# Maxima over the partitions: from a GpSimd instruction to a transposition, a row maximum and a product with ones

## The chip, the cores and the metric

One NeuronCore of a Trainium2 chip runs the whole program. Its engines are TensorE (PE in the profile), VectorE (DVE), ScalarE (ACT), GpSimd (POOL) and SyncE (SP), which only issues DMAs. They run side by side and meet at semaphores and at the barriers between blocks of code. The metric is the device time of one execution in microseconds.

## The reference

64 images of 224x224 are cut into 16x16 patches and projected to 196 tokens of 192 numbers. With a class token each image has 197 rows; 12,608 rows in all. Then come one attention layer with 12 heads, whose tensors are all rounded to 8-bit steps, and a layer of 8 experts (2 chosen per row):

```python
def fake_quant(x, n_bits=8):
    qmax = 2 ** (n_bits - 1) - 1
    scale = jnp.maximum(jnp.max(jnp.abs(x)) / qmax, 1e-08)
    q = jnp.clip(jnp.round(x / scale), -qmax - 1, qmax) * scale
    return x + jax.lax.stop_gradient(q - x)
...
qkv = jnp.einsum('bnc,oc->bno', fake_quant(x), fake_quant(w_qkv)) + b_qkv
attn = jnp.einsum('bhnd,bhmd->bhnm', fake_quant(q), fake_quant(k)) * scale
attn = jax.nn.softmax(attn, axis=-1)
out = jnp.einsum('bhnm,bhmd->bhnd', fake_quant(attn), fake_quant(v))
out = jnp.einsum('bnc,oc->bno', fake_quant(out), fake_quant(w_proj)) + b_proj
```

Each `fake_quant` needs one number: the largest absolute value of a whole tensor. On the chip a tensor lies over 128 partitions, so its maximum is first one number per partition, and then has to become one number that every partition knows. This last step is what the change is about. It is done four times, for eight numbers: three at once (input rows, two weight matrices), three at once (q, k, v), one (the smallest sum of exponentials, which sets the largest softmax value), one (the attention output).

## The kernel before

The program is a row of blocks with a barrier between each and the next:

- `embed`: patches to rows. GpSimd orders patches, TensorE transposes and multiplies.
- `normalise`: layer norm statistics, the first three maxima, rounding of weights (lines 560 to 637), then the rows are turned and q, k, v are computed once only for their maxima (`channels` on TensorE, `maxima` on VectorE), then the second three maxima.
- `attend_maxima`, called the score stage here: for 32 pairs of images ("couples") it makes q, k, v again, rounds q and k to integers on GpSimd (line 763), stores them, and computes all scores once, for the maximum and the sum of exponentials of every row. The second buffer lets couple n+1 be prepared during couple n.
- the first block of `attend`, called the shift block here: logarithms of the sums become a shift per row (line 1098), split in three bf16 parts (lines 1109 to 1116), turned by TensorE and written into q's rows in DRAM by many small DMAs.
- the second block of `attend`, called the attention stage: scores again, exponentials on ScalarE (line 1351, four buffers), rounding to 1/127 steps in turn by VectorE and GpSimd (line 1173; GpSimd takes units 1, 3, 5, 7 and 8 of the ten of a couple), products with v on TensorE. The last unit of a couple that uses `k_ends` waits for GpSimd's line 1234. SyncE issues in this order: loads of couples 0 and 1, the placing of the shifts of couples 4 to 31 (lines 1205 to 1207), q and k of couple 2, and v of couple 2 after couple 0 is through (line 1191), 24 more placings (lines 1209 to 1212), couple 3, and so on.
- `last_stages`, called the last block: projection, residual and norm, the gate and lists of rows per expert, the experts on lists, the weighted sum and the last norm. Every engine has its own long sequence in this one block. GpSimd starts with `plan_start` (lines 1855 to 1858) and the constants of lines 1549 to 1560; TensorE starts with waits for the constants (`init`), for VectorE's rounded bias (`bch`, line 1770) and for the first integers (`oq`).

In each of the four places the maximum over the partitions is `partition_all_reduce` on GpSimd. It stands at lines 464, 466, 1062 and 1250; VectorE waits for it in lines 594, 676, 1121 and 1402. The order of instructions in every engine is the order of the source; nothing rearranges it. Where GpSimd's stream goes from ordinary instructions to this one or back, the built program holds a configuration instruction, `MODIFY_POOL_CONFIG`, in the profile under the line of the instruction that follows it.

## Time and profile before

| | us |
|---|---|
| median of three executions | 2142.77 |
| lowest, highest | 2141.11, 2146.48 |
| the profiled execution, its own time | 2143.66 |
| its span in the trace | 2141.9 |
| PE busy in the span | 1530.5 |
| DVE busy | 1482.1 |
| ACT busy | 1361.9 |
| POOL busy | 1175.8 |

The span is the time from the first to the last instruction that the profiler recorded; 1.76 us of the execution's own time lie around it. In the rows below a line ends, in square brackets, with how long the engine was idle before the instruction and what released it. "issue" there means that the engine waited for nothing that the profile shows. The letters q in POOLq or SPq mark the sequencer of an engine, that is, instructions that are not counted as busy. Blocks begin at about these times: `normalise` 345, score stage 496, shift block 1030, attention stage 1049.6, last block 1330.

### The profile page before, as it was taken

To read this page: it belongs to the slowest core of one execution; us is meant where nothing else is said; L and a number is where in the kernel's file an instruction comes from. 1 tells how busy PE (TensorE), PEld (TensorE's weight loads), DVE (VectorE), ACT (ScalarE), POOL (GpSimd) and SP (SyncE) were. 2 spreads that over 40 slices of the span, in tenths; PEclk is the share of its full clock that TensorE was granted. 3 is DMA by queue.
4 is the path that set the end of the run, shared out by engine and by line. 5 is a ranking of instruction groups with operands and counts; after the bars stand their busy time and mean duration, and the time that the engine had idled before them with its cause. 6 is when DMAs were issued, how large, how long until landed. Compare 5 with 4: busy or idle time off the path is not lost. (4 is left out here: it accounts for less than half of the span.)

```text
span 2141.9 us, 51815 instructions
## 1 busy us (share of the span) xinstructions
PE 1530.5 (71%) x12460; PEld 1033.5 (48%) x12461; DVE 1482.1 (69%) x3737; ACT 1361.9 (64%) x3884; POOL 1175.8 (55%) x1921
## 2 busy tenths in 40 slices
PE   1999993884555555555378986788873999993663
PEld 1999992441111111111134443445542998883553
DVE  0455556896777777777456665688876777775996
ACT  0222221543999999999589996677772776663553
POOL 2333330004666666666155554377775888875886
PEclk9999996896555555555555555555556999997776
DMA  5334421001222222222344453544433555553774
GB/s 172 155 160 183 159 92 35 1 0 38 80 72 82 79 72 84 77 73 91 67 125 143 143 150 113 150 154 154 156 122 117 143 140 144 143 165 119 233 223 136
DMA packets 183979, 254.09 MB, mean 119 GB/s; under 512 B 28154, under 2 KB 147243, under 8 KB 180208
## 3 DMA queue, kind: packets, MB, share of 16 engines
q1 hardware_dynamic: 136256, 192.53, 29.2%
q0 software_dynamic: 19840, 39.17, 5.1%
q10 hardware_dynamic: 27808, 21.50, 3.1%
q8 instruction: 34, 0.56, 0.1%
q14 instruction: 41, 0.34, 0.1%
HBM read 140.66 MB, written 107.86 MB: 116 GB/s over the span
## 5 line engine op out<-in xcount | busy, mean ns | idle before, releaser
L957 ACT ACTIVATE exps_summed<-s,neg_shift 128x197 f32<-128x197 f32 x1184 | 482.7, 478 | 41.3 <-POOL neg_shift L824 39.7
L994 DVE TENSOR_REDUCE score_max<-s 128x788 f32 (+2 forms) x320 | 284.7, 894 | 108.9 <-PE s L898 96.7
L957 ACT ACTIVATION_READ_ACCUMULATOR exps_summed<-s,neg_shift (+1 forms) x1184 | 304.3, 260 | 0.0
L1351 ACT ACTIVATE exps<-st,scalars 128x788 f32<-128x788 f32 (+1 forms) x320 | 246.8, 889 | 21.1 <-PE st L1264 17.2
L2029 POOL DMA_INDIRECT expert_sums<-y_tile,row_places x216 | 215.6, 998 | 58.8 <-issue 28.2
L361 PE MATMUL mm<-w_tok,x_transposed 128*112 128x192 f32 x1344 | 239.6, 329 | 0.0
L306 ACT COPY x_transposed<-tp 128x672 f32<-128x672 f32 x112 | 80.4, 718 | 241.2 <-PE tp L352 241.2
L338 POOL TENSOR_SCALAR x_patches<-x_tile 112x768 f32<-112x768 f32 x112 | 93.1, 832 | 223.5 <-PE tp L352 184.8
L361 PEld LDWEIGHTS mm<-w_tok,x_transposed 128*112 128x112 f32 x1344 | 215.5, 179 | 0.2
L898 PE MATMUL s<-k_int,qk_int 16*128 16x197 bf16 x768 | 98.7, 354 | 139.9 <-ACT exps_summed L957 127.0
L1173 POOL TENSOR_SCALAR probs<-exps 128x788 bf16<-128x788 f32 (+1 forms) x160 | 130.3, 821 | 99.3 <-ACT exps L1351 99.2
L1173 DVE TENSOR_SCALAR probs<-exps 128x788 bf16<-128x788 f32 (+1 forms) x160 | 94.3, 590 | 112.0 <-ACT exps L1351 79.0
L392 DVE TENSOR_TENSOR h_rows_all<-mm,posb 112x192 f32<-112x192 f32 (+1 forms) x112 | 40.0, 357 | 178.7 <-PE mm L361 128.9
L824 POOL TENSOR_TENSOR neg_shift<-score_max,neg_alpha 128x4 f32<-128x4 f32 (+1 forms) x320 | 63.9, 200 | 136.0 <-DVE score_max L994 118.6
L1573 POOL DMA_INDIRECT listed_rows<-z_rows_a,row_index x99 | 103.3, 1043 | 60.9 <-DVE row_index L1755 31.9
L898 PEld LDWEIGHTS s<-k_int,qk_int 16*128 16x128 bf16 x768 | 26.0, 106 | 225.9 <-ACT exps_summed L957 215.7
L2122 ACT ACTIVATE g<-dn,down_bias 128x256 f32<-128x256 f32 x216 | 90.6, 470 | 68.4 <-PE dn L2071 67.3
L979 DVE TENSOR_SCALAR qkv_y<-pqk,scalars 128x394 f32<-128x394 f32 (+1 forms) x192 | 116.7, 608 | 24.5 <-POOL qk_int L763 21.3
L763 POOL TENSOR_SCALAR qk_int<-qkv_y,scalars 128x394 bf16<-128x394 f32 x96 | 122.4, 1275 | 17.9 <-issue 6.8
L2267 PE MATMUL weighted<-sum_a,weight_diagonals 128*128 128x192 f32 (+1 forms) x198 | 70.4, 449 | 83.6 <-DVE weight_diagonals L2321 60.2
L1573 POOL DMA_INDIRECT listed_rows<-z_rows_b,row_index x99 | 101.1, 1021 | 30.2 <-issue 27.8
L352 PE MATMUL tp<-ident_f,x_patches 112*128 112x112 f32 x672 | 85.1, 264 | 44.6 <-POOL x_patches L338 44.6
(403 smaller groups left out, 4561.9 us busy)
## 6 DMA issues: line engine op xcount, KB each, us to landing
x_tile<-in_x SPq DMA_DIRECT2D x24, 1568.0 KB
z_tile<-listed_rows SPq DMA_DIRECT2D x108, 196.0 KB
v_ints<-v_slots SPq DMA_DIRECT2D x32, 480.0 KB, 2.5
v_slots_in<-v_ints SPq DMA_DIRECT2D x32, 480.0 KB, 3.6
q_ints<-qk_int SPq DMA_DIRECT2D x32, 295.5 KB, 2.6
k_ints<-k_int SPq DMA_DIRECT2D x32, 295.5 KB, 2.5
q_shifted<-q_ints SPq DMA_DIRECT2D x32, 295.5 KB, 3.8
k_ones<-k_ints SPq DMA_DIRECT2D x32, 295.5 KB, 4.6
```

The costliest lines, as they stand in the source:

```text
L338: pool.tensor_scalar(xs[:, w % 2, :].rearrange("p (f w) -> p f w", w=PATCH), src, 1.0, 0.0, ALU.mult, ALU.add).then_inc(xs_ready, 1)
L361: last = nc.tensor.matmul(mm[w % 2][0:ROWS, 0:D], xt[:, w % 2, k * ROWS:(k + 1) * ROWS], w_tok[:, k, :], start=(k == 0), stop=(k == KCH - 1))
L763: pool.tensor_scalar(qk[:, s, g], y[:, g % 2], p.col(C_MQ), None, ALU.subtract).then_inc(used, 1)
L898: ins = nc.tensor.matmul(o[:, 2 * b + m, 0:SEQ], qk[lo:lo + HD, s, g, m * SEQ:m * SEQ + 128], kk[lo:lo + HD, s, g, m * SEQ:(m + 1) * SEQ], ...
L957: act.activation(gone[:, v % 2, k], ps[v % 3][:, k, 0:SEQ], ACT.Exp, scale=alpha, bias=nb[:, s, to:to + 1], accum_out=p.lsum[:, bass.ds(n ...
L979: dve.tensor_scalar(y[:, f % 2, 0:w], pqk[:, f % 2, 0:w], p.col(C_CQK if f < GRP else C_CV), p.col(C_MQ), ALU.mult, ALU.add).then_inc(y_re ...
L994: dve.tensor_reduce(columns(m, u), src, op=ALU.max, axis=AXL.X).then_inc(max_done, 1)
L1173: eng.tensor_scalar(pr[:, s, at(u):at(u) + size(u), 0:SEQ], ex[:, v % 4, 0:size(u)], 1.0, 128.0, ALU.mult, ALU.add).then_inc(sem, 1)
L1351: act.activation(ex[:, v % 4, 0:size(u)], src, ACT.Exp, scale=alpha, bias=p.col(C_LNSA)).then_inc(e_ready, 1)
L1573: pool.indirect_dma_start(p.zs[:, :], bass.IndirectOffsetOnAxis(ap=idx[0:rows, s, 4 * a + t:4 * a + t + 1], axis=0), z[0:rows, s, t, :], N ...
L2029: pool.indirect_dma_start(p.yD[:, :], bass.IndirectOffsetOnAxis(ap=to[:, k, t:t + 1].bitcast(U32), axis=0), y[:, k, t, :], None, bounds_ch ...
L2122: act.activation(g[:, k % 2, m], pd[k % 2][:, m], ACT.Gelu, scale=1.0 / WSCALE, bias=p.db[:, bass.ds(e * 2 + m, 1)]).then_inc(gs, 1)
```

## The change

Three helpers replace `partition_all_reduce`. `turn_maxima` has TensorE transpose the column of per-partition maxima (128 partitions by n) into n rows of 128 in PSUM. `reduce_maxima` has VectorE take the maximum of each row, and multiply an n by n identity with it, which gives a diagonal. `spread_maxima` has TensorE multiply a 3 by 128 tile of ones with that diagonal, so that all 128 partitions of PSUM hold the n maxima; the instruction on VectorE that used the result now reads it from PSUM. All four places are changed in this way, a PSUM bank is added in `normalise` and in the shift block, and GpSimd has no block of its own left in these two.

```diff
+def turn_maxima(nc, p, bank, values, n, sem):
+    nc.tensor.transpose(bank[0:n, 0:128], values, p.idf[:]).then_inc(sem, 1)
+
+def spread_maxima(nc, p, bank, n, sem):
+    nc.tensor.matmul(bank[:, 128:128 + n], p.ones3[0:n, :], p.diag[0:n, 0:n], start=True, stop=True).then_inc(sem, 1)
+
+def reduce_maxima(dve, p, bank, n, link, row):
+    link(dve.tensor_reduce(p.col(row, 0, n), bank[0:n, 0:128], op=ALU.max, axis=AXL.X))
+    link(dve.tensor_scalar(p.diag[0:n, 0:n], p.idf[0:n, 0:n], p.col(row, 0, n), None, ALU.mult))
...
+        self.ones3 = sb("ones_f32", [3, 128], f)
+        self.diag = sb("maxima_diagonal", [3, 3], f)
...
                 pool.tensor_copy(p.idb[:], p.idf[:]).then_inc(id_s, 1)
+                pool.memset(p.ones3[:], 1.0).then_inc(id_s, 1)
...
+        bank = p.ps("maxima", [128, 512], F32, c)
...
-            @block.gpsimd
-            def _(pool):
-                pool.wait_ge(max_ok, 1)
-                pool.partition_all_reduce(p.sc[:, C_ZMAX:C_ZMAX + 3], pm[:], 128, RMAX).then_inc(red, 1)
-                pool.wait_ge(max_ok, 2)
-                pool.partition_all_reduce(p.sc[:, C_QM:C_QM + 3], pm[:], 128, RMAX).then_inc(red2, 1)
...
             def _(pe):
+                pe.wait_ge(max_ok, 1)
+                turn_maxima(nc, p, bank, pm[:], 3, red)
+                pe.wait_ge(max_ok, 2)
+                spread_maxima(nc, p, bank, 3, red)
                 pe.wait_ge(w_ok, 1)
...
                     channels(NG - 1, d)
+                pe.wait_ge(max_ok, 3)
+                turn_maxima(nc, p, bank, pm[:], 3, red2)
+                pe.wait_ge(max_ok, 4)
+                spread_maxima(nc, p, bank, 3, red2)
...
                 dve.wait_ge(red, 1)
-                link(dve.tensor_scalar(p.sc[:, C_SX:C_SX + 3], p.sc[:, C_ZMAX:C_ZMAX + 3], 1.0 / QMAX, FLOOR, ALU.mult, ALU.max))
+                reduce_maxima(dve, p, bank, 3, link, C_TOP)
+                dve.sem_inc(max_ok, 1)
+                dve.wait_ge(red, 2)
+                link(dve.tensor_scalar(p.sc[:, C_SX:C_SX + 3], bank[:, 128:131], 1.0 / QMAX, FLOOR, ALU.mult, ALU.max))
...
+            bank = p.ps("smallest", [128, 512], F32, c)
...
-                @block.gpsimd
-                def _(pool):
-                    pool.wait_ge(low, 1)
-                    pool.partition_all_reduce(p.col(C_LMIN), p.col(C_TMP), 128, RMAX).then_inc(red, 1)
...
                 def _(pe):
+                    pe.wait_ge(low, 1)
+                    turn_maxima(nc, p, bank, p.col(C_TMP), 1, red)
+                    pe.wait_ge(low, 2)
+                    spread_maxima(nc, p, bank, 1, red)
                     for j, (lo, hi) in enumerate(spans):
...
                     link(dve.reciprocal(p.col(C_IALPHA), p.col(C_NALPHA)))
+                    dve.wait_ge(red, 1)
+                    reduce_maxima(dve, p, bank, 1, link, C_TOP)
+                    dve.sem_inc(low, 1)
                     for j, (lo, hi) in enumerate(spans):
...
-                            dve.wait_ge(red, 1)
+                            dve.wait_ge(red, 2)
-                            link(dve.tensor_scalar(p.col(C_TMP), p.col(C_LMIN), -1.0, None, ALU.mult))
+                            link(dve.tensor_scalar(p.col(C_TMP), bank[:, 128:129], -1.0, None, ALU.mult))
...
                     for sem in over:
                         pool.sem_clear(sem)
-                    pool.wait_ge(chain, 2)
-                    pool.partition_all_reduce(p.col(C_OM), p.col(C_TMP), 128, RMAX).then_inc(red, 1)
...
                     products_high(COUPLES - 1, 1)
+                    pe.wait_ge(chain, 2)
+                    turn_maxima(nc, p, pb, p.col(C_TMP), 1, red)
+                    pe.wait_ge(chain, 4)
+                    spread_maxima(nc, p, pb, 1, red)
...
                     dve.wait_ge(red, 1)
-                    quantise_inverse(dve, link, p.col(C_SO), p.col(C_IO), p.col(C_OM))
+                    reduce_maxima(dve, p, pb, 1, link, C_TOP)
+                    dve.wait_ge(red, 2)
+                    quantise_inverse(dve, link, p.col(C_SO), p.col(C_IO), pb[:, 128:129])
```

In the shift block ScalarE's `act.wait_ge(low, 2)` becomes `low, 3`, and VectorE's transposed-row maximum stands ahead of line 1098.

The first place is GpSimd's stream at the start of the score stage. Before:

```order
87 L771 COPY x_ends<-xq_t 128x2x60
88 L770 COPY x_ends<-xq_t 67x128
89 L771 COPY x_ends<-xq_t 67x2x60
90 L763 ISA
91 L763 TENSOR_SCALAR qk_int<-qkv_y,scalars 128x394 x3
92 L778 TENSOR_TENSOR q_ends<-qk_int,q_rows 128x3x4x5 x2
```

After:

```order
83 L798 COPY x_ends<-xq_t 128x2x60
84 L797 COPY x_ends<-xq_t 67x128
85 L798 COPY x_ends<-xq_t 67x2x60
86 L790 TENSOR_SCALAR qk_int<-qkv_y,scalars 128x394 x3
87 L805 TENSOR_TENSOR q_ends<-qk_int,q_rows 128x3x4x5 x2
```

L763 is now L790. The `ISA` row ahead of the rounding to integers, the configuration instruction, is gone; the other rows are the same.

The second place is GpSimd's stream from the end of the attention stage to the start of the last block. The 56 rows in one are the clearing of semaphores. Before:

```order
344 L1248 ISA x56
345 L1250 ISA
346 L1250 ISA scalars<-scalars 128x1
347 L1176 UNCONDITIONAL_BRANCH
348 L2438 UNCONDITIONAL_BRANCH
349 L1855 ISA
350 L1855 IOTA tile_number 1x108
351 L1856 MEMSET pad_rows 128x392
```

After:

```order
333 L1203 TENSOR_SCALAR probs<-exps 128x4x197
334 L1278 ISA x56
335 L1206 UNCONDITIONAL_BRANCH
336 L2472 UNCONDITIONAL_BRANCH
337 L1889 IOTA tile_number 1x108
338 L1890 MEMSET pad_rows 128x392
339 L1892 MEMSET pad_rows 128x2
```

Three `ISA` rows are gone: the configuration, the reduction itself, and the configuration ahead of `tile_number`. At the start of the attention stage the row ahead of `k_ends<-k_ones,k_rows` (L1234, now L1264) is gone in the same way, and in the shift block nothing of GpSimd is left.

The third place is VectorE at the end of the attention stage, where the maximum of the output is made. Before:

```order
1075 L1380 TENSOR_REDUCE out_max<-channels_t 128x1
1076 L1400 TENSOR_REDUCE scalars<-out_max 128x1
1077 L1401 TENSOR_SCALAR scalars<-scalars 128x1
1078 L182 TENSOR_SCALAR scalars<-scalars 128x1
1079 L183 RECIPROCAL scalars<-scalars 128x1
1080 L1404 TENSOR_TENSOR scalars<-scalars 128x1
```

After:

```order
1082 L1432 TENSOR_REDUCE scalars<-out_max 128x1
1083 L1433 TENSOR_SCALAR scalars<-scalars 128x1
1084 L198 TENSOR_REDUCE scalars<-po_rest 1x1
1085 L199 TENSOR_SCALAR maxima_diagonal<-ident_f,scalars 1x1
1086 L182 TENSOR_SCALAR scalars<-po_rest 128x1
1087 L183 RECIPROCAL scalars<-scalars 128x1
```

Two instructions stand between the last one before the reduction (L1401, now L1433) and its first user (L182): the row maximum, which waits for TensorE's transposition, and the diagonal, for which TensorE's product waits. `po_rest` is the PSUM tile that this place shares. The other three places have the same two rows.

## Rows read from the trace of the kernel before

Times are microseconds from the start of the span; L763 is line 763 of the kernel before.

**Rows 1.** The page: the chain of waits that ended last, by engine.
```profile
PE 17%; DVE 7%; issue 5%; POOL 4%; DMA 3%; ACT 1%; DVEq 0%; SPq 0%; POOLq 0%; ACTq 0%
```

**Rows 2.** The chain in order of time: start, duration (us), what; its longest piece.
```profile
1330.27 7.85 issue
```

**Rows 3.** By line: GpSimd's configuration instructions (ns, then first to last start, us).
```profile
L763 POOLq MODIFY_POOL_CONFIG  x2: 8/8/8, 503.9 to 503.9; - x2
L1855 POOLq MODIFY_POOL_CONFIG  x2: 11/11/11, 1330.2 to 1330.3; - x2
```

**Rows 4.** Timeline: start, duration (us), instruction, [idle before and releaser].
```profile
363.97 0.17 DVE L595 TENSOR_SCALAR scalars<-scalars 128x3 f32<-128x3 f32 x1 [0.61 <-POOL scalars L464]
...
493.23 0.23 DVE L678 TENSOR_SCALAR scalars<-scalars 128x3 f32<-128x3 f32 x1 [0.56 <-POOL scalars L466]
```

**Rows 5.** Timeline at the start of the score stage.
```profile
510.64 3.81 POOL L763 TENSOR_SCALAR qk_int<-qkv_y,scalars 128x394 bf16<-128x394 f32 x3 [6.76 <-issue]
```

**Rows 6.** Timeline at the start of the shift block.
```profile
1031.81 0.15 DVE L1093 TENSOR_SCALAR scalars<-scalars 128x1 f32<-128x1 f32 x1
1032.61 0.37 DVE L1098 SCALAR_TENSOR_TENSOR shift<-shift,scalars,score_max 128x148 f32<-128x148 f32 x1 [0.35 <-DVE scalars L1095]
1035.05 0.16 DVE L1111 CAST last_parts<-shift_rest 128x4 bf16<-128x4 f32 x1
1035.32 0.09 PEld L1085 LDWEIGHTS last_t<-ident_bf,last_parts 128*12 128x12 bf16 x1 [9.12 <-DVEq L1116]
1036.81 0.15 DVE L1123 TENSOR_SCALAR scalars<-scalars 128x1 f32<-128x1 f32 x1
```

**Rows 7.** Timeline of the first image pairs of the attention stage.
```profile
1054.04 4.15 ACT L1351 ACTIVATE exps<-st,scalars 128x788 f32<-128x788 f32 x5 [2.62 <-PE st L1264]
1060.59 0.53 POOL L1234 TENSOR_TENSOR k_ends<-k_ones,k_rows 128x60 bf16<-128x60 bf16 x2 [10.04 <-issue]
...
1062.05 4.46 ACT L1351 ACTIVATE exps<-st,scalars 128x788 f32<-128x788 f32 x6 [3.87 <-POOL probs L1173]
```

**Rows 8.** Timeline, later: SyncE's DMA issues and TensorE.
```profile
1066.85 0.43 SPq L1189 DMA_DIRECT2D k_ones<-k_ints  x1
...
1072.33 0.33 SPq L1192 DMA_DIRECT2D v_slots_in<-v_ints  x1
1072.70 12.23 SPq L1031 DMA_DIRECT2D q_ints<-shift_last  x24
...
1089.09 0.85 PE L1264 MATMUL st<-q_shifted,k_ones 32*128 32x197 bf16 x12 [7.86 <-DMA k_ones<-k_ints]
```

**Rows 9.** Timeline at the end of attention.
```profile
1325.49 0.21 DVE L1401 TENSOR_SCALAR scalars<-scalars 128x1 f32<-128x1 f32 x1
1328.72 0.15 DVE L182 TENSOR_SCALAR scalars<-scalars 128x1 f32<-128x1 f32 x1 [3.01 <-POOL scalars L1250]
```

**Rows 10.** Timeline at the start of the last block.
```profile
1335.77 0.41 DVE L1770 SCALAR_TENSOR_TENSOR w_proj_q<-b_proj_parts,ident_f 3x192 bf16<-3x192 bf16 x1
1340.63 0.29 POOL L1560 TENSOR_SCALAR_AFFINE_SELECT lower_index<-lower_index 128x64 f32<-128x64 f32 x1
1341.18 0.32 PE L1630 MATMUL proj<-w_proj_q,o_int 128*128 128x192 bf16 x1 [18.25 <-POOL lower_index L1560]
```

**Rows 11.** Timeline: prices of a row maximum, a transposition, small products.
```profile
360.39 0.27 DVE L583 TENSOR_REDUCE class_stats<-row_tmp 112x1 f32<-112x112 f32 x1
...
1349.85 0.48 PE L1677 MATMUL z_tp<-ident_f,z_rows_a 128*128 128x128 f32 x1 [0.98 <-ACT z_rows_a L1603]
...
1358.12 1.77 PE L1645 MATMUL gate_l<-gate_w,gate_hidden 96*128 96x8 f32 x8
```

**Rows 12.** Stretches: busy us (instructions) of each engine, granted clock, DMA share.
```profile
369.70:391.00 21.30, 16.80 (x73) 10.60 (x74) 15.32 (x40) 10.26 (x22) 0.00 (x0) 0.51 0.01 1
391.00:493.00 102.00, 81.49 (x489) 45.45 (x487) 99.65 (x176) 42.48 (x87) 0.17 (x1) 1.00 0.00 1
493.00:1640.00 1147.00, 757.22 (x6680) 338.92 (x6680) 820.36 (x1967) 931.00 (x3022) 695.12 (x1371) 0.50 0.34 107
```

More of the change, by code:

```diff
@@ L239 @@
  C_IQ, C_IK, C_IV, C_CQ, C_CK, C_CV, C_ALPHA, C_NALPHA, C_LMIN, C_SA, C_LNSA, C_IALPHA, C_SAV, C_OM, C_SO,
- C_IO, C_CO, C_SOUT, C_TMP, C_MQ, C_CQK, C_MIN, C_EPS, C_ISOUT, C_ONES) = range(41)
+ C_IO, C_CO, C_SOUT, C_TMP, C_MQ, C_CQK, C_MIN, C_EPS, C_ISOUT, C_ONES, C_TOP) = range(42)
 def embed(p):
@@ L676, in _ @@
                 dve.wait_ge(red2, 1)
+                reduce_maxima(dve, p, bank, 3, link, C_TOP)
+                dve.sem_inc(max_ok, 1)
+                dve.wait_ge(red2, 2)
                 s3 = p.sc[:, C_SQ:C_SQ + 3]
-                link(dve.tensor_scalar(s3, p.sc[:, C_QM:C_QM + 3], p.col(C_SXW), 1.0 / QMAX, ALU.mult, ALU.mult))
+                link(dve.tensor_scalar(s3, bank[:, 128:131], p.col(C_SXW), 1.0 / QMAX, ALU.mult, ALU.mult))
                 link(dve.tensor_scalar(s3, s3, FLOOR, None, ALU.max))
@@ L1073, in _ @@
                             place_last(act, a, k, 1, 0, at_first[1])
-                    act.wait_ge(low, 2)
+                    act.wait_ge(low, 3)
                     act.activation(p.col(C_LNSA), p.col(C_SA), ACT.Ln).then_inc(lnd, 1)
```

## The prediction, made before the run

> **What bounds the kernel now.** I read the page first: no engine is busy all through, so what matters is what is waited for at each place. The chain of waits that ended last gives PE 17%, DVE 7% and "issue" 5% [rows 1], and of its pieces the longest is of the last kind: 7.85 us from 1330.27 [rows 2], right behind a configuration instruction of GpSimd at 1330.2 to 1330.3 [rows 3]. So I read GpSimd's configuration instructions by line, then the timeline around each, and last the other waits for the reduction. A configuration instruction shows 8 to 11 ns [rows 3], but behind it GpSimd stands still for some 7 to 10 us, and the profile names no releaser [rows 2, 5, 7]. The reader is to look for who is behind GpSimd in each place: that alone is time.
>
> **Part by part.** Everything is in the time of the profiled execution, 2143.66 us.
>
> (a) Start of the score stage. GpSimd has copied the row ends at 503.9, has its configuration instruction then [rows 3], and starts to round q and k at 510.64, 6.76 us later with "issue" as reason [rows 5]. All that follows (k's DMAs, the first scores, the first exponentials on ScalarE) hangs on these three roundings. "issue" says that its input was there; VectorE's first two results do not wait for GpSimd, so nothing else is late when the stall goes: -6.76. Bounds: -7.0 (the whole of it and the start of the next) and -5 (if the third input, which needs a buffer back from GpSimd, comes late once the roundings run close).
>
> (b) Start of the attention stage. `k_ends` is at 1060.59, after 10.04 us of "issue" behind the configuration instruction of line 1234 [rows 7]. Its input k has landed before 1054, since ScalarE's first exponential of scores made from it starts at 1054.04 [rows 7]. ScalarE does five exponentials and then has no free buffer, since GpSimd has not rounded its unit: it waits 3.87 us, until 1062.05 [rows 7]. Without the stall GpSimd's `k_ends` (0.53) is done near 1054, before its first rounding is due, so ScalarE's wait goes: -3.87. What is late next? TensorE waits 7.86 us for couple 3's k at 1089.09 [rows 8]. That looks like an end that would swallow the gain. But SyncE's v load at 1072.33 is issued when couple 0's last product is through, 24 placings then take 12.23 us, and only then couple 3 is loaded [rows 8]. That product comes 3.87 earlier, so this chain moves with it, unless SyncE becomes late by itself: its load of couple 2's k is over at 1066.85 + 0.43 = 1067.28, 5.05 us ahead of 1072.33, so 3.87 fits [rows 8]. I take -3.87; bounds 0 (all swallowed) and -5.0 (up to where SyncE itself sets the time).
>
> (c) Start of the last block. GpSimd's constants end at 1340.63 + 0.29 = 1340.92, and TensorE starts at 1341.18 for that reason [rows 10]. The stall ends at 1330.27 + 7.85 = 1338.12 [rows 2], so 2.8 us of work stand behind it. Without it they end near 1333.1. Then VectorE's bias chain is last: it ends at 1335.77 + 0.41 = 1336.18 [rows 10], and TensorE can start 0.1 later, at 1336.3. So -4.9, not -7.85. Everything behind it (projection, norm, gate, lists) is relative to this start.
>
> (d) The round trip that is added. No row shows it whole, so I add it from pieces at TensorE's lower clock of 1.2 GHz, which holds in three of the four places [rows 12]: VectorE's end to TensorE's start 0.11 (1035.21 to 1035.32, [rows 6]); a transposition with 128 columns of f32 0.48 [rows 11]; back 0.05; maximum of 128 elements 0.27 (112 elements, [rows 11]) and link 0.04; the diagonal 0.21, as for another one-column product with a scalar from memory [rows 9], and link 0.04; to TensorE 0.11; a product of few columns 0.25 (eight take 1.77, [rows 11]); back 0.05. The sum is 1.61. Bounds: 1.2 if the pieces overlap (clock at 2.4 GHz, weight load before the wait ends), 2.6 if every crossing costs 0.3 us more than its nearest row, as the 0.35 at line 1098 shows that waits can [rows 6]. This is set against what VectorE waits now:
> - first maxima: 0.61 now [rows 4], so +1.00. Here the configuration had been done while VectorE worked, nothing is gained there.
> - second maxima, at the higher clock: 1.61 - 0.21 for the transposition = 1.40 against 0.56 [rows 4]: +0.84.
> - end of attention: VectorE ends at 1325.70 and goes on at 1328.72, a wait of 3.01 that also holds the tail of a configuration [rows 9]. 3.02 - 1.61: -1.41.
> - shift block: now VectorE goes from line 1120 to 1123 (1036.81) without an idle [rows 6], the reduction costs nothing. After the change VectorE waits for the transposition before line 1098: from 1031.96, 0.11 + 0.48 + 0.05 + 0.31 + 0.25 gives 1033.16, and with the wait for the logarithm checked after it some 0.15 more, against 1032.61: +0.70. Behind this wait in VectorE's queue are all of the block's splits, and TensorE's turns and the DMAs wait for those, so it counts in full. The product with ones lies beside VectorE's splits, as does ScalarE's wait for `low`.
>
> (e) The memset of the ones (about 0.1) lies before GpSimd's first wait for the patches; the two PSUM banks cost no time.
>
> Sum: -6.76 - 3.87 - 4.9 + 1.00 + 0.84 - 1.41 + 0.70 = -14.4. From 2143.66 this gives 2129.3. The median shown is 0.9 lower than the profiled execution; from it I get 2128.4, and I say **2128.5**.
>
> Two rules of the Trainium skill speak to this. In this trace the gaps from the configuration to the next work are 6.7, 10.0 and 7.9 us for (a), (b) and (c) [rows 3, 5, 7, 10]. The page "GPSIMD Engine Reference", section "Instruction dispatch", puts the first call to a freshly loaded kernel at about 6 us (5.95). By that figure 0.8 us of (a)'s gap would be something else and might stay, and the sum would be -13.6; in (b) and (c) there would still be enough time, as another end is reached first. And the same page's "When to use GPSIMD" names GpSimd as the only option for a reduction across partitions, which speaks against the whole change; for the instruction alone the trace agrees (0.56 to 0.61 us of waiting against an estimate of 1.4 to 1.6), and the change would then be a loss of 0.8 to 1.0 at each place if the configuration cost nothing.
>
> **Rivals.**
> 1. The attention stage takes the gain of (b) back: SyncE's DMA issues or the landing of couple 2's and 3's k are the real end. For it: TensorE waits 7.86 us for k at 1089.09 [rows 8]. Against it: the issue before that wait is itself released by TensorE. (b) is then 0, or the round trips come near their upper bound (4 x 1.0): sum -10.5, and both together -6.5. Time 2132 to 2136.
> 2. The stalls move instead of going: GpSimd needs a configuration for another instruction in place of these (`iota`, the masks, the power in the last norm). Against it: the order after the change shows no such row, and `iota` stands there among ordinary instructions. If one stall of 7 us stayed: -7.5, time 2135.
> 3. More than forecast: SyncE issues its placings behind an earlier start and (b) reaches -5.0, the round trips cost 1.2 (-1.6), and stages after it are met earlier by DMAs: -17 or more, time 2126 and below.
> 4. Slower than before: the clock. TensorE runs `normalise` from 369.7 to 391 at half clock and from 391 to 493 at full [rows 12]. The two small products now come before its block work, and if the rise came late or not at all, TensorE would bound this stage: 81.5 us of its busy time in 102 would become 163, so up to +61, or 0.6 us lost for each us that the rise is late. From a rise 24 us later on this outweighs the 14.4, and with none the time is 2143.7 - 14.4 + 61 = 2190. Against it: the rise came after 21 us of dense work, the new products are two small ones ahead of it, and nothing of the dense work changes.
>
> **How the numbers follow.** The forecast has 0.66, rival 1 0.17, rival 2 0.04, rival 3 0.09, rival 4 0.02; 0.02 are left for a run-to-run difference that hides it. The three executions before lie 5.4 us apart, so the median itself is uncertain by some 2 us. A measurement of this kernel can tell about 0.3%, 6.4 us, from no change: faster means below 2136.3. Forecast, rival 1's larger part and rival 3 lie there, 0.92; within 0.3%: 0.05; slower 0.03. The forecast's own range, from the bounds of (d) (+1.6 to -1.6 for four places, and +4.0 at worst) and the executions' spread, is 2124 to 2133; to hold 8 in 10 I take in most of rival 1 and some of rival 3: 2122 to 2135.
>
> **What would show it.** In the profile after the change: no configuration instruction after the first few us; the rounding to integers starting within 0.3 us of the last copy of row ends; no wait of ScalarE for GpSimd near the sixth exponential of the attention stage, and couple 3's first score some 3.9 us nearer to the stage's start; TensorE's first projection released by VectorE's line 1770 (now 1804), about 6.0 us after the block's start (1330.3 before) instead of 10.9; VectorE's pause before its user of the maximum near 1.6 us in all where it was 0.61, 0.56 and 3.01, and the first line of the shift split 0.7 later. The forecast is wrong if couple 3 starts at the same distance from the stage's start, if a pause around a maximum is above 2.6 us, or if the granted clock rises elsewhere.

## The result, and the profile after

| | before | after |
|---|---|---|
| median (executions) | 2144.85 us (8) | 2127.80 us (8) |
| lowest, highest | 2140.43, 2148.04 | 2122.70, 2136.76 |
| profiled execution, its span | 2143.66, 2141.9 | 2127.63, 2125.9 |

The ratio is 0.9926, with a 95% interval of 0.9911 to 0.9942: faster by 0.74%, 16 us at 2144.85 (the two medians are 17.0 apart). The forecast was 2128.5, from a difference of 14.4.

The two timelines, cut at the same instructions; "again" is a second profile of the same changed kernel, from a later comparison (E5):

| stretch, us | before | after | again | forecast change |
|---|---|---|---|---|
| start to normalise's class statistics | 355.8 | 353.0 | 356.5 | 0 |
| to the first scale (holds the first maxima) | 8.2 | 9.4 | 9.3 | +1.00 |
| to the last row maximum of normalise | 127.4 | 126.4 | 128.5 | 0 |
| to the second scale (second maxima) | 1.8 | 2.7 | 3.1 | +0.84 |
| score stage: GpSimd's first memset to its first q integers | 14.15 | 8.05 | 8.05 | -6.76 |
| q integers to the shift block | 519.8 | 518.8 | 518.8 | 0 |
| shift block to its first shift line | 2.2 | 2.8 | 2.8 | +0.70 |
| attention stage: first memset to the output's maximum | 275.6 | 270.9 | 270.1 | -3.87 |
| output's maximum to its scale | 3.5 | 2.3 | 2.2 | -1.41 |
| to TensorE's first projection | 12.5 | 7.9 | 7.9 | -4.9 |
| projection to the end | 800.7 | 803.5 | 803.2 | 0 |

Two stretches between these rows are not shown, 3.3 us ahead of the score stage and 17 us behind the first shift line; they differ by 0.4 at most. The seven rows with a forecast add to -13.8 in the first profile and to -14.4 in the second. The rows without one differ by up to 3.5 us between two profiles of one kernel (353.0 and 356.5), so the -16.0 of the spans is -13.8 and scatter. Part of the scatter is TensorE's clock: in the second profile it was granted at half between 482 and 488 us, in the first at full there, and the stretch to the last row maximum is 128.5 us in place of 126.4.

By line, GpSimd's configuration instructions. One pair is left, at the program's start; those of [rows 3] at lines 763 and 1855 are gone, and so are the ones that the kernel before has at lines 464, 1062, 1234 and 1250:

```profile
L335 POOLq MODIFY_POOL_CONFIG  x2: 11/11/11, 1.1 to 1.2; - x2
```

Timeline (start, duration, instruction, [idle before and releaser]) at the start of the score stage, the place of [rows 5]:

```profile
495.21 5.83 DVE L997 CAST k_int<-scalars 128x1182 bf16<-128x1182 f32 x2
...
497.12 3.29 POOL L780 MEMSET v_slots<- 128x3840 bf16 x1
...
501.10 0.51 PE L889 MATMUL pqk<-xq_t,w_slots 128*128 128x394 bf16 x1 [9.60 <-DVE k_int L997]
...
502.85 3.80 POOL L790 TENSOR_SCALAR qk_int<-qkv_y,scalars 128x394 bf16<-128x394 f32 x3 [0.69 <-DVE qkv_y L1006]
```

The 6.76 us of "issue" are gone. What GpSimd waits for now is VectorE's first result, 0.69. That is late because TensorE waited for VectorE's two casts, which take 5.83 us here.

ScalarE, SyncE and TensorE in the first image pairs of the attention stage, answering to [rows 7, 8]. The first line is TensorE's wait for couple 2's k in the kernel before:

```profile
1073.26 1.02 PE L1264 MATMUL st<-q_shifted,k_ones 32*128 32x197 bf16 x12 [0.61 <-DMA k_ones<-k_ints]
```

The changed kernel:

```profile
1045.68 14.47 ACT L1383 ACTIVATE exps<-st,scalars 128x788 f32<-128x788 f32 x19 [2.56 <-PE st L1292]
...
1060.00 0.33 SPq L1222 DMA_DIRECT2D v_slots_in<-v_ints  x1
1060.37 11.82 SPq L1058 DMA_DIRECT2D q_ints<-shift_last  x24
...
1064.18 0.85 PE L1292 MATMUL st<-q_shifted,k_ones 32*128 32x197 bf16 x12 [3.86 <-DMA k_ones<-k_ints]
...
1076.09 0.84 PE L1292 MATMUL st<-q_shifted,k_ones 32*128 32x197 bf16 x12 [4.20 <-DMA k_ones<-k_ints]
```

ScalarE does 19 exponentials in a row; before, it did 5 and then waited 3.87 us for GpSimd. SyncE's v load comes 18.7 us after the stage's start at 1041.3, where it was 1072.33 - 1049.6 = 22.7. The 24 placings follow as before, and couple 3 starts 34.8 after the start, where it was 39.5. TensorE's waits for k are now 3.86 us for couple 2 and 4.20 for couple 3, where they were 0.61 and 7.86. So TensorE does wait longer for couple 2, but couple 3 sets the time, and it comes sooner.

The pauses around the maxima on VectorE, first and second place, answering to [rows 4]:

```profile
360.44 0.15 DVE L613 TENSOR_TENSOR partition_max<-partition_max,class_stats 64x1 f32<-64x1 f32 x1
...
362.37 0.16 DVE L619 TENSOR_SCALAR scalars<-maxima 128x3 f32<-128x3 f32 x1 [0.73 <-PE maxima L193]
...
489.90 0.16 DVE L698 TENSOR_TENSOR partition_max<-class_stats 128x1 f32<-128x1 f32 x1
...
491.54 0.22 DVE L705 TENSOR_SCALAR scalars<-maxima,scalars 128x3 f32<-128x3 f32 x1 [0.53 <-PE maxima L193]
```

From the end of the last line ahead of each pause to its user VectorE has 362.37 - 360.59 = 1.78 us and 491.54 - 490.06 = 1.48 us, where it waited 0.61 and 0.56.

The same at the end of attention, with TensorE, answering to [rows 9]:

```profile
1312.50 0.21 DVE L1433 TENSOR_SCALAR scalars<-scalars 128x1 f32<-128x1 f32 x1
1312.77 0.37 PE L188 MATMUL po_rest<-ident_f,scalars 128*1 128x128 f32 x1 [2.83 <-DVE scalars L1433]
1313.25 0.28 DVE L198 TENSOR_REDUCE scalars<-po_rest 1x1 f32<-1x128 f32 x1 [0.54 <-PE po_rest L188]
1313.56 0.20 DVE L199 TENSOR_SCALAR maxima_diagonal<-ident_f,scalars 1x1 f32<-1x1 f32 x1
1313.82 0.58 PE L193 MATMUL po_rest<-maxima_diagonal,ones_f 1*128 1x1 f32 x2 [0.68 <-DVE maxima_diagonal L199]
1314.51 0.16 DVE L182 TENSOR_SCALAR scalars<-po_rest 128x1 f32<-128x1 f32 x1 [0.75 <-PE po_rest L193]
```

From 1312.71 to 1314.51: 1.80 us, where it was 3.02. The product with ones is two passes (x2), 0.58 us.

VectorE in the shift block, answering to [rows 6]:

```profile
1023.03 0.15 DVE L1120 TENSOR_SCALAR scalars<-scalars 128x1 f32<-128x1 f32 x1
...
1024.45 0.37 DVE L1128 SCALAR_TENSOR_TENSOR shift<-shift,scalars,score_max 128x148 f32<-128x148 f32 x1 [0.16 <-DVE maxima_diagonal L199]
```

The first shift line comes 1.27 us after the line before the pause; in [rows 6] it was 0.65. The added 0.62 is what the row maximum and the diagonal hold VectorE.

The start of the last block, answering to [rows 10]:

```profile
1317.17 0.51 DVE L1723 TENSOR_SCALAR o_y<-channels_t,scalars 128x512 f32<-128x512 f32 x1
1317.60 0.47 DVE L1724 TENSOR_SCALAR o_y<-channels_t,scalars 64x512 f32<-64x512 f32 x1
...
1319.29 0.37 POOL L1594 TENSOR_SCALAR_AFFINE_SELECT lower_index<-lower_index 128x64 f32<-128x64 f32 x1
...
1321.92 0.41 DVE L1804 SCALAR_TENSOR_TENSOR w_proj_q<-b_proj_parts,ident_f 3x192 bf16<-3x192 bf16 x1
1322.43 0.32 PE L1664 MATMUL proj<-w_proj_q,o_int 128*128 128x192 bf16 x1 [8.03 <-DVE w_proj_q L1804]
```

GpSimd's constants end at 1319.66, 2.8 us before TensorE starts, and VectorE's bias chain releases TensorE now. From the output's scale to the end of that chain it is 7.8 us, where it was 7.5: the two roundings in it (lines 1727 and 1728) take 0.51 and 0.63 us in place of 0.43 and 0.41, with GpSimd writing its constants beside them. E4 has the same two times; E1 to E3, where the constants come later, have 0.43 and 0.41.

The first stretch of [rows 12] (busy us and instructions of PE, PEld, DVE, ACT, POOL; granted clock; DMA share; GB/s):

```profile
369.70:391.00 21.30, 16.07 (x78) 10.08 (x78) 16.07 (x41) 11.39 (x24) 0.00 (x0) 0.62 0.01 1
```

The clock rose somewhat sooner: 0.62 of full in this stretch against 0.51 makes some 5 us, of which 1.6 are the earlier first scale. Rival 4, a late rise, did not occur.

### The profile page after: what moved, and what is told of

It is laid out like the page before. It is cut to its first block and busy times, and to the rows that moved or that the text cites. A ratio compares the mean times of both kernels' runs of the same rounds, so it can differ in the third digit from the quotient of the medians.

```text
span 2125.9 us, 51836 instructions
## 1 busy us (share of the span) xinstructions
PE 1531.2 (72%) x12472; PEld 1032.7 (49%) x12473; DVE 1486.6 (70%) x3745; ACT 1361.7 (64%) x3884; POOL 1176.2 (55%) x1918
## 5 line engine op out<-in xcount | busy, mean ns | idle before, releaser
L790 POOL TENSOR_SCALAR qk_int<-qkv_y,scalars 128x394 bf16<-128x394 f32 x96 | 122.4, 1275 | 11.8 <-DVE qkv_y L1006 5.7
L1006 DVE TENSOR_SCALAR qkv_y<-pqk,scalars 128x394 f32<-128x394 f32 (+1 forms) x192 | 116.7, 608 | 14.8 <-POOL qk_int L790 11.5
```

Of the source, the lines that this page charges most:

```text
L790: pool.tensor_scalar(qk[:, s, g], y[:, g % 2], p.col(C_MQ), None, ALU.subtract).then_inc(used, 1)
L1006: dve.tensor_scalar(y[:, f % 2, 0:w], pqk[:, f % 2, 0:w], p.col(C_CQK if f < GRP else C_CV), p.col(C_MQ), ALU.mult, ALU.add).then_inc(y_re ...
```

## Experiments

Theory: the gain is GpSimd's standstill behind a configuration instruction, and it counts in each place by what is queued behind it; the round trips cost about 1 us each. Rivals: the gain comes from the removed instruction itself or from the clock; the parts act only together; SyncE's order takes it back.

E1 to E4 ran on one chip, against 31 executions of the kernel before with a median of 2306.06 us. On that chip every kernel is some 160 us longer, and in the four profiles taken there this lies behind TensorE's first projection: in E3's it is at 1336.0 us and the rest takes 966 us, against 801. The stretches ahead of it match the other profiles, with the exceptions told under E4, so I read these four by stretch, and their ratios within the chip.

**E1, the instruction back, its result unused.**

```diff
+                pool.wait_ge(max_ok, 1)
+                pool.partition_all_reduce(p.unused[:], p.idf[:, 0:3], 128, RMAX).then_inc(spare, 1)
...
```

> The changed kernel, but GpSimd also runs a partition_all_reduce of a constant at each of the four old places, and nobody uses or waits for its result; the maxima still go by TensorE and VectorE. Theory (the gain is the configuration instruction that GpSimd meets when it returns to ordinary work while someone is queued behind it): MODIFY_POOL_CONFIG comes back at the first q integers of the score stage, at the first k_ends of the attention stage and at the start of the last block, each with some 6 to 7 us of wait; the three markers grow by 6, 4.6 and 4.5 us, the round trips stay as in the changed kernel, so about +15 us over it: 2143, ratio to the kernel before 0.997 to 1.003. Rival (the gain is the removed instruction and its wait for the maxima, or the clock): the time stays near 2128, ratio 0.993.

Ratio 0.9995 (0.9982 to 1.0008). GpSimd's timeline:

```profile
512.99 3.81 POOL L799 TENSOR_SCALAR qk_int<-qkv_y,scalars 128x394 bf16<-128x394 f32 x3 [7.45 <-issue]
...
1063.87 0.53 POOL L1278 TENSOR_TENSOR k_ends<-k_ones,k_rows 128x60 bf16<-128x60 bf16 x2 [10.47 <-issue]
...
1339.38 0.22 POOL L1905 IOTA tile_number<- 1x108 f32 x1 [8.54 <-issue]
```

The three standstills are back (7.45, 10.47 and 8.54 us), with nobody waiting for a result. From stage start to q integers 14.8 us; attention stage 274.7; output scale to first projection 13.3. The whole gain is gone, though the new way is all there: neither the wait for the reduction's result nor the clock is the gain. This run brings back the reduction together with the configuration, so it doesn't part the two; E10 below does. In the second of the three standstills, not all is the configuration: `k_ends` also needs k, as it does in [rows 7]. TensorE's first scores in the kernel before, made from the same k, start 7.1 us ahead of the `k_ends` of 1060.59:

```profile
1053.48 0.84 PE L1264 MATMUL st<-q_shifted,k_ones 32*128 32x197 bf16 x12 [5.51 <-DMA k_ones<-k_ints]
```

**E2, E3, E4, one part at a time.** The new way stands in normalise's two places alone (E2), in the shift block alone (E3), or at the end of attention alone (E4, whose edit is shown); the others keep `partition_all_reduce`.

```diff
-                    pool.partition_all_reduce(p.col(C_OM), p.col(C_TMP), 128, RMAX).then_inc(red, 1)
+                    pe.wait_ge(chain, 2)
+                    turn_maxima(nc, p, pb, p.col(C_TMP), 1, red)
+                    pe.wait_ge(chain, 4)
+                    spread_maxima(nc, p, pb, 1, red)
```

> The kernel before with the new way only in the two places of normalise. Theory: the score stage starts 6.1 us sooner, the two maxima cost 1.2 and 0.9 us more, net -4.0 us: 2141, ratio 0.998; the configuration waits of the attention stage and of the last block are as before. Rival: the parts act together (GpSimd needs to be free of the old instruction altogether), nothing is gained here: 2145 or, with the dearer maxima, 2147.

Ratio 0.9977 (0.9961 to 0.9993). GpSimd's first q integers follow its copies without an idle, 7.3 us after the stage's start:

```profile
503.50 3.82 POOL L790 TENSOR_SCALAR qk_int<-qkv_y,scalars 128x394 bf16<-128x394 f32 x3
```

> The kernel before with the new way only in the shift block. Theory: the attention stage's first couples are 4.6 us shorter, the shift block 0.65 us longer, net -4.0 us: 2141, ratio 0.998. Rival (SyncE's order sets the first couples, and what ScalarE gains it waits again for couple 2's k): the attention stage is shorter by under 1 us, net 0: 2145, ratio 1.000.

Ratio 0.9974 (0.9958 to 0.9990). The attention stage takes 270.5 us; `k_ends` comes with its data. TensorE at couple 3:

```profile
1081.60 0.85 PE L1287 MATMUL st<-q_shifted,k_ones 32*128 32x197 bf16 x12 [4.57 <-DMA k_ones<-k_ints]
```

The wait was 7.86 in [rows 8]. SyncE's order did not swallow the gain, but it leaves 4.57. In this run GpSimd's standstill at the start of the last block, which the edit doesn't touch, is the longest:

```profile
1332.91 0.22 POOL L1878 IOTA tile_number<- 1x108 f32 x1 [11.99 <-issue]
```

Its configuration instruction is at 1322.53, 10.4 us before; in [rows 2, 3] it is 7.9 us. From output scale to projection E3 has 15.0 us, where the kernel before has 12.5. Why this one took longer was not found.

> The kernel before with the new way only at the end of the attention stage. Theory: the pause for the attention output's maximum is 1.8 us instead of 3.0, and the last block's first projection comes 4.5 us sooner, net -5.7 us: 2139, ratio 0.9973. Rival (TensorE's start in the last block waits for something else by then): only the 1.2 us of the pause, 2143.5, ratio 0.9995.

Ratio 0.9969 (0.9953 to 0.9986). VectorE's scale and TensorE's first projection:

```profile
1326.85 0.16 DVE L182 TENSOR_SCALAR scalars<-po_rest 128x1 f32<-128x1 f32 x1 [0.75 <-PE po_rest L193]
...
1334.77 0.32 PE L1655 MATMUL proj<-w_proj_q,o_int 128*128 128x192 bf16 x1 [8.03 <-DVE w_proj_q L1795]
```

From output scale to projection 7.9 us. The three ratios multiply to 0.9922; the whole change gave 0.9926 and, below, 0.9932. Each of the three has an interval of about 0.0016 to either side, so the parts add as far as these times can tell. Each stretch is shorter only where its own part is done. The others stay within 1 us, but for a standstill that can take longer by itself: the 15.0 us in E3.

E5 to E8 ran on a chip on which the kernel before has a median of 2145.86 us (11 executions).

**E5, the changed kernel again** (no edit).

> The changed kernel once more, as the yardstick for the three beside it. Theory: ratio to the kernel before 0.992 to 0.9935, if the four places act one by one (the product of the parts tried alone, with their round trips, is 0.992). Rival (the parts overlap): 0.990 or 0.995.

2132.09 us, ratio 0.9932 (0.9915 to 0.9948), inside what was expected. Its stretches are in the table above.

**E6, GpSimd's long memset later.**

```diff
-                pool.memset(vs[:], 0.0).then_inc(zero, 1)
...
                 stamps(0, 0)
+                pool.memset(vs[:], 0.0).then_inc(zero, 1)
+                pool.wait_ge(zero, 5)
```

> The changed kernel with GpSimd's memset of v_slots (3.29 us) moved behind the first three integer steps of the score stage. Theory (what is left of the start is VectorE's two casts, 5.83 us instead of 2.08 because they run beside GpSimd's memsets): the casts fall to 2 to 3 us, TensorE's first product comes at about 2.6 us after the stage's start instead of 6.3, and the first q integers about 3.6 us sooner, -3.5 us over the changed kernel, ratio to before 0.991. Rival (the casts are slow for another reason, as the read of one broadcast column): they stay at 5.8 us and nothing moves but GpSimd's own memset, 0 us.

2129.05 us, ratio 0.9926 (0.9913 to 0.9939). VectorE's casts and GpSimd's integers:

```profile
496.15 2.61 DVE L998 CAST k_int<-scalars 128x1182 bf16<-128x1182 f32 x2
...
500.56 3.81 POOL L789 TENSOR_SCALAR qk_int<-qkv_y,scalars 128x394 bf16<-128x394 f32 x3 [0.69 <-DVE qkv_y L1007]
```

The casts fall from 5.83 to 2.61 us and the q integers come 3.2 us sooner (4.8 after the start). But the first exponential of the stage comes only 1.9 sooner (16.2 after the start against 18.1), since GpSimd's v values and first shifts now stand behind the memset; the whole from stage start to shift block is 525.6 against 526.8. The mechanism is right, but nearly two thirds of its gain are given back, and the times of E5 and E6 can't be told apart.

**E7, couples 2 and 3 asked for earlier.**

```diff
+                    place_rows((0, 1))
+                    load_qk(1, 0)
+                    place_rows((2, 3))
+                    place_lasts((0,))
+                    load_v(1, 0)
+                    load_qk(1, 1)
+                    place_lasts((1, 2, 3))
+                    load_v(1, 1)
```

> The changed kernel with SyncE's order changed in the attention stage: q and k of couple 2 are asked for after half of the placings, q and k of couple 3 before 18 of the last 24. Theory (after the change SyncE's order is the next bound of these first couples): the waits of 3.86 and 4.20 us for k_ones before couples 2 and 3 go, -7 to -8 us over the changed kernel, ratio to before 0.989. Rival (the placings that now come later are waited for before couple 4, or the other engines can't follow): the two waits move to couple 4, gain under 2 us, 0.992.

2127.72 us, ratio 0.9920 (0.9907 to 0.9933). Between the two: the attention stage is 267.1, 3.0 to 3.8 shorter than in the two profiles of the changed kernel. Couple 2's wait is gone. SyncE and TensorE for couples 3 and 4:

```profile
1068.35 0.43 SPq L1223 DMA_DIRECT2D k_ones<-k_ints  x1
...
1075.55 0.84 PE L1309 MATMUL st<-q_shifted,k_ones 32*128 32x197 bf16 x12 [2.48 <-DMA k_ones<-k_ints]
...
1085.52 0.85 PE L1309 MATMUL st<-q_shifted,k_ones 32*128 32x197 bf16 x12 [2.27 <-DMA k_ones<-k_ints]
```

k of couple 3 is asked for at 1068.35 and is there at 1075.55: 7.2 us, where the changed kernel has 1072.65 to 1076.09, 3.4. The load stands among the placings' DMAs; that these make it land late is likely, but was not tried by itself. Couple 4, which needs all placings, has a wait that it did not have. SyncE's order was the next bound, but it can be moved only in part.

**E8, first maxima by GpSimd, a memset behind.**

```diff
+                pool.partition_all_reduce(p.sc[:, C_ZMAX:C_ZMAX + 3], pm[:], 128, RMAX).then_inc(red, 1)
+                pool.memset(p.unused[:], 0.0).then_inc(spare, 1)
```

> The changed kernel, but the first three maxima come from partition_all_reduce on GpSimd again, with a small memset right behind it, while GpSimd has 130 us of nothing ahead. Theory (the configuration costs only where ordinary work is queued behind it): MODIFY_POOL_CONFIG is back in normalise, but nobody waits; the pause of VectorE before the first scale is 0.6 us instead of 1.78; the score stage starts as in the changed kernel; -1.2 us, ratio 0.992. Rival (the configuration is paid once more at the next ordinary instruction after a barrier): the score stage is 6 us later again, ratio 0.995.

2132.45 us, ratio 0.9939 (0.9926 to 0.9952). What was expected of the memset was wrong:

```profile
361.96 0.39 POOL L485 PARTITION_ALL_REDUCE scalars<-partition_max  x1 [38.35 <-DVEq L617]
362.22 0.17 POOL L486 MEMSET unused_max<- 128x3 f32 x1
...
362.38 0.17 DVE L619 TENSOR_SCALAR scalars<-scalars 128x3 f32<-128x3 f32 x1 [0.62 <-POOL scalars L485]
...
509.90 3.81 POOL L790 TENSOR_SCALAR qk_int<-qkv_y,scalars 128x394 bf16<-128x394 f32 x3 [6.83 <-issue]
```

VectorE's pause is 0.62 as expected, but the memset ran at once, 0.26 us behind the start of the reduction, and the configuration is by line in front of the q integers again:

```profile
L790 POOLq MODIFY_POOL_CONFIG  x2: 10/10/10, 503.1 to 503.1; - x2
```

So a memset does not bring the configuration back, and the 6.83 us are paid as before.

**E10, the same with a small tensor_scalar behind** (with E9 on a chip where the kernel before has 2143.43 us).

```diff
-                pool.memset(p.unused[:], 0.0).then_inc(spare, 1)
+                pool.tensor_scalar(p.unused[:], p.idf[:, 0:3], 1.0, None, ALU.mult).then_inc(spare, 1)
```

> The first maxima by partition_all_reduce as in the hybrid before, but the small instruction behind it is a tensor_scalar of three columns instead of a memset. In that hybrid the memset ran at once and the configuration stayed in front of the first q integers. Theory (a memset and a copy run in either configuration, a tensor_scalar needs the one it was built for): the configuration now stands in front of the small tensor_scalar, some 6 us inside GpSimd's 130 us of nothing, the score stage starts 8.1 us after its barrier as in the changed kernel, VectorE's first pause stays 0.6 us; -1.2 us over the changed kernel, ratio to before 0.992. Rival (it is loaded again at the first long instruction of each block): the score stage starts 14 us after its barrier, ratio 0.9945.

2128.26 us, ratio 0.9921 (0.9908 to 0.9934). GpSimd's timeline:

```profile
361.44 0.39 POOL L485 PARTITION_ALL_REDUCE scalars<-partition_max  x1 [38.36 <-DVEq L617]
368.91 0.79 POOL L486 TENSOR_SCALAR unused_max<-ident_f 128x3 f32<-128x3 f32 x1 [7.08 <-issue]
...
503.47 3.80 POOL L790 TENSOR_SCALAR qk_int<-qkv_y,scalars 128x394 bf16<-128x394 f32 x3
```

Now the standstill of 7.08 us lies in GpSimd's idle time, and the integers start 7.4 us after the stage's start with no idle. With it the reduction is there and the gain is too: the price is not the reduction, but who is queued behind the configuration. The old instruction can stay in a place if the way back is made early. The pause of 0.61 against 1.78 us at the first maxima is seen in the timeline, not in the times, whose interval is wider than that.

**E9, a version made of what was found.** ScalarE writes the ones of `k_int` and the zeros of `v_slots`, the loads are ordered as in E7, the gate's weights come after the last couple, GpSimd writes the ones of `o_int`.

```diff
+                for s in range(2):
+                    act.activation(kk[:, s].rearrange("p g t -> p (g t)"),
+                                   p.col(C_ONES).broadcast_to([128, GRP * 2 * SEQ]), ACT.Copy).then_inc(filled, 1)
+                for s in range(2):
+                    act.activation(vs[:, s], p.col(C_ONES).broadcast_to([128, VW]), ACT.Copy, scale=0.0).then_inc(filled, 1)
...
-        link(dve.memset(oq1[D1:KB], 1.0))
```

> The changed kernel with four more edits: ScalarE, idle there, writes the ones of k_int and the zeros of v_slots at the start of the score stage (VectorE's casts and GpSimd's long memset go); SyncE asks for q and k of couples 2 and 3 earlier, as tried before, and for the gate's weights only after the last couple's loads instead of before the placings; GpSimd writes the ones of o_int in the last block. Theory (the next bounds are those the runs showed: GpSimd's and VectorE's fills, SyncE's order, VectorE's bias chain): first q integers 4.5 us sooner than in the changed kernel, attention stage 4 to 7 us shorter (the waits of 2.5 us before couple 3 and 2.3 us before couple 4 that the earlier order left shrink, since the placings start 3.5 us sooner), last block 0.9 us sooner; together -9 to -12 us, ratio to before 0.987 to 0.9885. Rival (only moved: ScalarE's fills reach into its first exponentials, the loads stay behind the placings in the DMA queue): -4 us, 0.9905.

2117.14 us, ratio 0.9877 (0.9859 to 0.9895). It beats the kernel before by 1.2% and the changed kernel too, whose intervals (0.9911 to 0.9942 and 0.9915 to 0.9948) lie above. Rows of ScalarE and GpSimd at the start of the score stage, and of VectorE at the start of the last block:

```profile
499.79 2.27 ACT L974 ACTIVATE k_int<-scalars 128x1182 bf16<-128x1182 f32 x2 [25.98 <-PEq L467]
...
502.14 3.80 POOL L789 TENSOR_SCALAR qk_int<-qkv_y,scalars 128x394 bf16<-128x394 f32 x3
...
1312.17 0.84 DVE L1743 TENSOR_SCALAR o_y<-channels_t,scalars 128x512 f32<-128x512 f32 x1 [0.54 <-PEq L1207]
1312.93 1.06 DVE L1744 TENSOR_SCALAR o_y<-channels_t,scalars 64x512 f32<-64x512 f32 x1
```

The q integers start 2.9 us after the stage's start (8.1 in the changed kernel), and 4.7 of the 5.2 us are left at the shift block (522.1 against 526.8). The attention stage is 267.3, 2.8 to 3.6 shorter than in the changed kernel, less than the 4 to 7 expected; asking for the gate's weights later only changed where the waits are (2.84 before couple 3, 1.44 before couple 4). The last block gained nothing: VectorE's memset of 0.91 is gone, but its next two instructions take 0.84 and 1.06 us in place of 0.51 and 0.47, 0.92 more in all, beside GpSimd's memsets. These stretches hold 7 to 8 us; the median lies 10.5 to 12 below the changed kernel's, and where the rest is was not found.

## Why the prediction was right

The mechanism and the sum were right: -14.4 forecast, -13.8 and -14.4 in two profiles. E1 to E4 and E10 show that it was for the reasons given. That the time itself came within 0.7 us of 2128.5 is in part luck: the median before that it was counted from, 2142.77 of three executions, is 2144.85 with eight, and some steps came out larger and some smaller than forecast. By its steps:

- **(a) score stage**, -6.76 forecast, -6.1 measured at the q integers in both profiles. The standstill went whole (E2: 14.15 to 7.30, 6.85). The forecast said that nothing else would be late, and that the rounding would start within 0.3 us of the last copy; it was 0.69, for VectorE's first result. The neighbour that was overlooked is the cast of `k_int`, 2.08 us before and 5.83 after. What it costs doesn't last: from the stage's start to the shift block it is 533.9 us before and 526.8 in both profiles, -7.1, and 526.7 in E2, where the q integers are 0.75 sooner.
- **(b) attention stage**, -3.87 forecast, -4.7 and -5.5 measured, the second beyond the bound of -5.0 (E3 has -5.1). The chain was as told: ScalarE's wait goes, couple 0's product and with it SyncE's v load come 4.0 sooner, 24 placings, couple 3. The rest of the first profile's 4.7: the placings take 11.82 in place of 12.23, and couple 3's k is there 3.4 us after it is asked for, 0.3 less. Rival 1 did not occur: TensorE's wait for couple 2's k grew by 3.3 us and couple 2 comes only 0.8 sooner after the stage's start, but couple 3, behind which no such wait follows, comes 4.7 sooner. E7 shows its resource as the next bound.
- **(c) last block**, -4.9 forecast, -4.5 measured, released by the bias chain as forecast. The chain is 0.36 longer beside GpSimd's constants, which the step had left out.
- **(d) round trip**, 1.61 forecast, 1.78, 1.48 and 1.80 measured in the first profile, 1.78, 1.79 and 1.71 in the second. The second place was reckoned at the full clock, 1.40; in the second profile the clock had fallen back to half by the time of the product with ones (0.58 us there, 0.38 in the first), so this place is dearer than forecast, +0.91 and +1.23 for +0.84. The pieces differ more than the sum: transposition 0.37 (0.48 forecast), product with ones 0.58 (0.25 forecast, as one pass; the rows show two). The shift block has +0.62, +0.70 forecast. That GpSimd's instruction is the quicker one by itself is right too: 0.62 in E8, 0.61 in E10.
- **The old pause at the end of attention.** The way to the reduction needs a configuration too. It is at 1322.59 in the kernel before, and the reduction starts 5.6 us later, 2.5 after its input:

```profile
1328.23 0.38 POOL L1250 PARTITION_ALL_REDUCE scalars<-scalars  x1 [9.04 <-issue]
```

  This tail, which the step named, is why VectorE's pause was 3.01 there and 0.6 in normalise, and why the round trip by itself is a gain in this place alone.
- **The clock.** One sign of being wrong was a clock that rises elsewhere. It rose some 3 us sooner after the first scale (23.6 and 23.8 us in the two profiles, 26.6 before), which is neither the late rise of rival 4 nor quite the same place. The stretch it lies in is 127.4 us before, 126.4 and 128.5 after, so no gain can be read from it.

The Trainium skill, "GPSIMD Engine Reference", section "Instruction dispatch", has about 6 us for a first call after a load. The standstills here are 6.8 to 12.0 us in the rows shown, some with a barrier or a wait for k in them; in E10, where nothing else can hold GpSimd, it is 7.08, about 1 us above the page's figure. In place (a) the whole gap went (E2), and nothing of it was left over as the sum by that figure would have it.

## What to carry to other kernels

An engine's reconfiguration costs what is queued behind it, and it is paid on the way to the special instruction (5.6 us here) and again when the engine goes back to ordinary work (about 7, once 10.4), often a block later than the instruction that caused it: look in the timeline for "issue" gaps of GpSimd behind such an instruction, and for who waits there. Either take out all of the instructions that need it, or make the way back early, with an instruction that really needs the other configuration. When a stall goes, look at what starts beside another engine for the first time.

## What was not expected of the hardware

**Fills on VectorE and GpSimd shut each other out.** VectorE's two casts (1182 columns of f32 to bf16 each) stand beside GpSimd's memsets in each profile but E9's. In the kernel before VectorE won, and GpSimd's two memsets took 1.15 us each:

```profile
496.91 2.08 DVE L970 CAST k_int<-scalars 128x1182 bf16<-128x1182 f32 x2
...
497.22 1.15 POOL L750 MEMSET x_ends<- 128x512 bf16 x1
498.31 1.15 POOL L751 MEMSET x_ends<- 67x512 bf16 x1
```

In the changed kernel the same memsets take 0.53 us each and the casts 5.83 together. That is the sum of 2.08, 0.46 (the spacing of the small memsets) and 3.29, the whole memset of `v_slots`. By the single casts it is the same: the second takes 3.98 us, and 0.76 in E6, where that memset comes later. In E2, with the starts at the same distance within 0.02 us, the casts took 2.61 and the memset of `v_slots` 3.93. The Trainium skill, "SBUF — State Buffer", section "Who interferes with whom", says that a cast on VectorE can take a port pair that it shares with GpSimd, for the whole instruction, and that the one that is first blocks the other fully. The traces agree in the sizes: what is lost is a whole instruction of the neighbour. What decides who is first stays open: the small memsets took 1.15 in all profiles with a `partition_all_reduce` in normalise (E1, E3, E4, E8 and, with the configuration back long before, E10) and 0.53 in all without, so it is not the configuration in force.

**Not every GpSimd instruction needs the configuration.** A memset and a copy ran in the one of the reduction (E8); for a tensor_scalar, `k_ends`' tensor_tensor and `iota` it was loaded.

**Chips differ in one part of a program.** Behind TensorE's first projection it is 961 to 966 us on one chip (four kernels) and 799 to 804 on the others, in a part that none of the edits touches but E9's; what lies ahead agrees within 5 us for the same edits. The cause was not looked for.
